# Expert outputs scattered by addition into one memory row per token, with a fence op, a ring of eight and rows cleared by copies

## What is computed

```
x = layernorm(x + self_attention(x))            # 16 heads, one shared key and value head
x = layernorm(x + cross_attention(x, context))  # one head, additive mask
x = layernorm(x + ffn(x))                       # 8 experts, the best 2 for each token

ffn:  scores = softmax(x @ Wg.T);  the two largest, divided by their sum, are the weights comb
      for each expert e:  h = x @ W1[e].T + b1[e];  a, b = split(h)
                          g = a * sigmoid(b)                       # 512 numbers per token
                          out += (g @ Wo.T + bo) * comb[e]
```

## Time and profile before

| | before |
|---|---|
| median of 3 runs | 1420.98 us |
| the profiled execution, its own time | 1420.46 us |
| its span, first to last instruction | 1418.7 us |
| busy: PE, DVE, ACT, POOL | 1274.8, 1147.8, 747.3, 642.5 us |
| moved by DMA | 237.57 MB, mean 167 GB/s |
| mean granted clock of TensorE | 0.974 |

### The profile page before, as it was taken

How to read it: one execution, slowest core, us unless ns; L and a number is a source line. 1 busy time by engine, 2 the same in 40 slices (tenths; PEclk the granted TensorE clock), 3 DMA queues, 4 the chain that set the end, 5 groups by cost and what they waited for, 6 DMA issues and landing times.

```text
span 1418.7 us, 30148 instructions
## 1 busy us (share of the span) xinstructions
PE 1274.8 (90%) x7734; PEld 900.7 (63%) x7735; DVE 1147.8 (81%) x3145; ACT 747.3 (53%) x1740; POOL 642.5 (45%) x978
## 2 busy tenths in 40 slices
PE   6997999999999999999988569999999999968886
PEld 4443555655556555555553357888888888858886
DVE  0565889898888988988986658888888888869998
ACT  1245777777777787777776212233233223314444
POOL 3011354455444554555445323333333333348886
PEclk9998999999999999999999679999999999989999
DMA  7656667667676675775655853433443344379995
GB/s 163 166 111 125 113 151 172 149 163 149 158 157 140 146 163 135 157 138 145 157 129 195 290 215 129 135 130 129 134 135 129 130 134 135 133 271 330 332 335 194
DMA packets 182817, 237.57 MB, mean 167 GB/s; under 512 B 21376, under 2 KB 144256, under 8 KB 176960
## 3 DMA queue, kind: packets, MB, share of 16 engines
q1 hardware_dynamic: 158864, 169.50, 47.3%
q0 software_dynamic: 17488, 55.02, 10.3%
q10 hardware_dynamic: 6368, 11.89, 2.4%
HBM read 138.34 MB, written 98.30 MB: 167 GB/s over the span
## 4 chain that ended last, share of the span: by engine, by line
PE 62%; DVE 17%; issue 9%; DMA 5%; ACT 4%; POOL 1%; SPq 1%; DVEq 0%; ACTq 0%; POOLq 0%
PE psO L623 6%; PE psS L730 5%; PE psHb L1399 5%; PE psHb L1396 5%; PE psHb L1395 4%; PE psHa L1395 4%; PE psHa L1396 4%; PE psHa L1399 4%; PE psB L652 4%; PE psT L740 4%; DVE negmax L1031 3%; DVE x2in L1591 3%; PE psX L1419 2%; DVE gt_lo L1567 2%; PE psA L612 2%
## 5 line engine op out<-in xcount | busy, mean ns | idle before, releaser
L1031 DVE TENSOR_REDUCE negmax<-psS 128x2 f32<-128x512 f32 x512 | 350.7, 688 | 94.6 <-PE psS L730 77.0
L870 ACT ACTIVATE probs<-psT 128x512 f32<-128x512 f32 x512 | 304.0, 599 | 161.0 <-PE psT L740 143.3
L1476 ACT ACTIVATE sig<-hb 128x512 f32<-128x512 f32 x135 | 85.6, 634 | 286.6 <-DVE hb L1549 286.6
L730 PE MATMUL psS<-kstack,qstack 96*128 96x256 bf16 x1024 | 195.2, 273 | 31.3 <-DVE kstack L1129 15.6
L740 PE MATMUL psT<-qstack,kstack 99*128 99x512 bf16 x512 | 194.8, 383 | 4.4 <-ACT probs L870 4.3
L1358 POOL DMA_INDIRECT g_rows<-g,slot x135 | 134.7, 998 | 69.8 <-issue 66.5
L730 PEld LDWEIGHTS psS<-kstack,qstack 96*128 96x128 bf16 x1024 | 93.1, 104 | 90.2 <-DVE negmax L1031 27.4
L482 POOL DMA_INDIRECT lists<-x,slots x128 | 128.6, 1005 | 33.9 <-issue 30.1
L623 PE MATMUL psO<-probs,vaug 128*32 128x512 f32 x1024 | 139.1, 616 | 0.4 <-ACT probs L870 0.4
L1560 DVE SCALAR_TENSOR_TENSOR g<-g,xe,sig 128x512 f32<-128x512 f32 x135 | 101.5, 752 | 26.0 <-DVE g L1556 16.6
L1549 DVE TENSOR_TENSOR hb<-psHb,b 128x512 f32<-128x512 f32 x135 | 93.4, 692 | 33.1 <-issue 28.9
(11 more groups left out here) (207 smaller groups left out, 2956.4 us busy)
## 6 DMA issues: line engine op xcount, KB each, us to landing
rows<-g_rows SPq DMA_DIRECT2D x32, 1024.0 KB, 8.1
qstack<-q_parts SPq DMA_DIRECT2D x192, 128.0 KB
xe<-lists SPq DMA_DIRECT2D x135, 133.0 KB, 2.1
q_parts<-qpart SPq DMA_DIRECT2D x32, 384.0 KB
sums<-x SPq DMA_DIRECT2D x32, 264.0 KB
x2in<-sums SPq DMA_DIRECT2D x32, 264.0 KB, 4.7
xt<-in_x_t SPq DMA_DIRECT2D x32, 256.0 KB
part_raw<-in_f_t SPq DMA_DIRECT2D x32, 256.0 KB, 5.0
```

The source lines that it names most:

```text
L730: last = mm(psS[:, u % 2, hh * S:(hh + 1) * S], qstack[0:KROWS, b1.s4, 2 * hp + hh, c * P:(c + 1) * P], kstack[0:KROWS, b1.s4, :], start=T ...
L870: nc.scalar.activation(probs[:, u % PT, :], psT[:, u % 2, :], ACT.Exp, scale=SELF_SCALE).then_inc(sm["exp_done"], 1)
L1031: v.tensor_reduce(negmax[:, b1.s2, 2 * hp:2 * hp + 2, c], psS[:, u % 2, :].rearrange("p (h k) -> p h k", h=2), AX.X, ALU.max, negate=True) ...
```

## The change

`g_rows` has one row per token now, and the scatter of a tile adds to it (`compute_op=ALU.add`) in place of overwriting it. From this follow the other parts:

1. The column with the first expert goes (`ROW` is `D + E + 1`), and with it the DVE copy L1160, POOL's `away` and DVE's wait for it. `slot` is a plain copy of the row number.
2. Two tiles of different experts can hold the same token. POOL waits before the scatter of tile o: for o = 1 to 7 until the scatters of the three tiles before it have landed, later only where the expert changes (`turn_tab`, 16 at such a tile and 0 otherwise, is loaded into a register and added to the number waited for). After the waits POOL runs a `fence` op on one column, then the scatter.
3. The rows must be zero at first. POOL clears a 128 x 512 tile `zeros`, SP writes it 4 times (1 MB) to `zero_rows` in step 0 of the attention stage, and ACT issues 20 copies of 1 MB from there to `g_rows`, one in unit 15 of each of the steps 6 to 25.
4. `xe` gets a ring of 8, and the loops of the tile stage are written out for 8 tiles in place of 4.
5. In the pair stage SP loads 512 KB of `rows` per pair, POOL adds nothing, and PE transposes `rows` itself.

The diff, cut to its core:

```
-            pool.iota(x2[:, s, :, D + E], pattern=[[2 * P, QC]], base=2 * s * S, channel_multiplier=2,
+            pool.iota(x2[:, s, :, D + E], pattern=[[P, QC]], base=s * S, channel_multiplier=1,
...
             if t.fixed and t.n == 0:
                 load_setup()
+                sp.wait_ge(dram["zeros_made"], 1)
+                sp.dma_start(dram["zero_rows"].rearrange("(p k) h -> p k h", p=P),
+                             zeros[:, :].unsqueeze(1).to_broadcast([P, ZROWS, zeros.shape[1]])
+                             ).then_inc(dram["zeros_stored"], 16)
...
+        def clear_rows(t):
+
+            places = dram["g_rows"].rearrange("(p k) h -> p (k h)", p=P)
+            width = ZROWS * dram["g_rows"].shape[1]
+            n = t.n - 6
+            if 0 <= n < places.shape[1] // width:
+                act.wait_ge(dram["zeros_stored"], 16)
+                act.dma_start(places[:, n * width:(n + 1) * width], dram["zero_rows"].rearrange("(p k) h -> p (k h)", p=P)
+                              ).then_inc(dram["rows_cleared"], 16)
...
+                if u == 15:
+                    clear_rows(t)
...
-                v.tensor_copy(x2[:, b6.s2, :, D + E + 1], topf[:, b6.s2, :, 0]).then_inc(sm["comb_ready"], 1)
...
             if active(t):
-                wait(sp, "g_ready", done(t.back(4)))
+                wait(sp, "g_ready", done(t.back(8)))
...
-            if active(t):
-
-                wait(pool, f"xe_loaded{t.s4}", ring(t) + 16)
+            turn = None
+            for m in range(1, 4):
+
+                before = o.back(m)
+                if active(o) and (not o.fixed or o.n >= 8):
+                    turn = pool.value_load(turn_tab[0:1, bass.ds(o.n, 1)], min_val=0, max_val=16) if turn is None else turn
+                    wait(pool, f"g_stored{before.s4}", ring(before) + turn)
+                elif active(o) and before.n >= 0:
+                    wait(pool, f"g_stored{before.s4}", ring(before) + 16)
+            if active(o):
                 wait(pool, "g_ready", done(o))
-                pool.tensor_tensor(away[:, t.s4:t.s4 + 1], xe[:, t.s4, FIRST:FIRST + 1],
-                                   expf[:, bass.ds(t.n, 1)], ALU.subtract).then_inc(sm["away_ready"], 1)
+                wait(pool, "fenced", done(o.back(4)))
+                pool.tensor_tensor(fence[:, o.s4:o.s4 + 1], zero[:, :], zero[:, :], ALU.add).then_inc(sm["fenced"], 1)
             if active(o):
                 pool.indirect_dma_start(out=dram["g_rows"], out_offset=bass.IndirectOffsetOnAxis(
-                    ap=slot[:, o.s4:o.s4 + 1], axis=0), in_=g[:, o.s4], in_offset=None
+                    ap=slot[:, o.s4:o.s4 + 1], axis=0), in_=g[:, o.s4], in_offset=None, compute_op=ALU.add
                     ).then_inc(sm[f"g_stored{o.s4}"], 16)
...
-            if active(t, PAIRS):
-                wait(pool, f"rows_loaded{t.s4}", ring(t) + 16)
-                for c in range(QC):
-                    wait(pool, "g_transposed", QC * t.n + c - 3)
-                    pool.tensor_tensor(row_sum[:, t.s2 * QC + c], rows[:, t.s4, c, 0:H], rows[:, t.s4, c, H:2 * H], ALU.add
-                                       ).then_inc(sm["rows_added"], 1)
...
                 if active(t, PAIRS):
-                    wait(pe, "rows_added", QC * t.n + c + 1)
+                    if c == 0:
+                        wait(pe, f"rows_loaded{t.s4}", ring(t) + 16)
...
-                v.scalar_tensor_tensor(slot[:, i.s4:i.s4 + 1], away[:, i.s4:i.s4 + 1], 0.0, xe[:, i.s4, ID:ID + 1],
-                                       ALU.not_equal, ALU.add)
+                v.tensor_copy(slot[:, i.s4:i.s4 + 1], xe[:, i.s8, ID:ID + 1])
...
-            "g_rows": nc.dram_tensor("g_rows", (2 * (T + 2 * E * P), H2 // 2), F32, kind="Internal").ap(),
+            "g_rows": nc.dram_tensor("g_rows", (T + 2 * E * P, H2 // 2), F32, kind="Internal").ap(),
+            "zero_rows": nc.dram_tensor("zero_rows", (4 * P, H2 // 2), F32, kind="Internal").ap(),
```

More of the change, by code:

```diff
@@ L70, in s4, with n, s8, back @@
         return self.r % 4
+class Tile(Step):
+    @property
+    def n(self):
+        return 8 * self.j + self.r
+    @property
+    def s8(self):
+        return self.r % 8
+    def back(self, k):
+        return Tile(self.j, self.r - k)
 def attention(nc, ctx, io, dram):
@@ L112, in attention @@
     rden = sb("rden", [P, 2, QC * 8])
-    with nc.sbuf_tensor("pad", [P, 2 * E, ROW], F32) as pad:
+    ZROWS = 4
+    with nc.sbuf_tensor("pad", [P, 2 * E, ROW], F32) as pad, nc.sbuf_tensor("zeros", [P, dram["g_rows"].shape[1]], F32) as zeros:
         pass
@@ L445, in expert_constants @@
             number, listbase, upper = dram["number"], dram["listbase"], dram["upper"]
+            pool.memset(zeros[:, :], 0.0).then_inc(dram["zeros_made"], 1)
             pool.memset(pad[:, :, :], 0.0).then_inc(sm["pool_chain"], 1)
@@ L1198, in experts @@
     I32 = mybir.dt.int32
-    rows, row_sum, x2in, y, result = (dram[k] for k in ("rows", "row_sum", "x2in", "y", "result"))
+    rows, x2in, y, result = (dram[k] for k in ("rows", "x2in", "y", "result"))
     w1_hi, w1_lo, b1, bo = dram["w1_hi"], dram["w1_lo"], dram["b1"], dram["bo"]
@@ L1215, in experts @@
         pass
+    with nc.sbuf_tensor("g", [P, 4, H], F32) as g:
+        pass
     past = sb("past", [P, TILES, E])
@@ L1221, in experts @@
     exp_tab = sb("exp_tab", [P, TILES], I32)
+    turn = sb("turn", [P, TILES])
+    turn_tab = sb("turn_tab", [P, TILES], I32)
     pad_tab = sb("pad_tab", [P, E], I32)
[L1224 to L1225 removed]
+    xe = sb("xe", [P, 8, ROW])
     sig = sb("sig", [P, 2, H])
@@ L1228, in experts @@
     xet_lo = sb("xet_lo", [P, 2, DC * P], F32R)
-    away = sb("away", [P, 4])
+    fence = sb("fence", [P, 4])
+    zero = sb("zero", [P, 1])
     slot = sb("slot", [P, 4], U32)
@@ L1267, in ring, with ring8 @@
     def ring(i):
-        return 16 * (i.j + i.r // 4)
+        return 16 * ((2 if isinstance(i, Tile) else 1) * i.j + i.r // 4)
+    def ring8(i):
+        return 16 * (i.j + i.r // 8)
     def active(i, count=TILES):
@@ L1274, in pipeline @@
     def pipeline(eng, step):
-        for r in range(8):
-            step(Step(0, r))
-        with eng.Fori(2, TILES // 4) as j:
-            for r in range(4):
-                step(Step(j, r))
-        for r in range(TILES % 4 + 3):
-            step(Step(TILES // 4, r))
+        for r in range(16):
+            step(Tile(0, r))
+        with eng.Fori(2, TILES // 8) as j:
+            for r in range(8):
+                step(Tile(j, r))
+        for r in range(TILES % 8 + 3):
+            step(Tile(TILES // 8, r))
     def pair_pipeline(eng, step):
@@ L1327, in load_rows @@
         def load_rows(t):
-            wait(sp, "rows_added", done(t.back(4), QC))
+            wait(sp, "g_transposed", done(t.back(4), QC))
             sp.dma_start(rows[:, t.s4], stored_rows[bass.ds(t.n, 1)].rearrange("o p c h -> (o p) c h")
@@ L1415, in step @@
             if active(t):
-                wait(pe, f"xe_loaded{t.s4}", ring(t) + 16)
+                wait(pe, f"xe_loaded{t.s8}", ring8(t) + 16)
                 wait(pe, "xet_split", done(t.back(2)))
                 for k in range(DC):
-                    last = nc.tensor.transpose(psX[:, t.s2, k * P:(k + 1) * P], xe[:, t.s4, k * P:(k + 1) * P],
+                    last = nc.tensor.transpose(psX[:, t.s2, k * P:(k + 1) * P], xe[:, t.s8, k * P:(k + 1) * P],
                                                ident[:, :])
@@ L1429, in step @@
                         lambda: None).then_inc(sm["a_product"], 1)
-            if active(i) and active(t) and t.r % 4 != 3:
+            if active(i) and active(t) and t.r % 8 != 7:
                 ahead.append(load_expert(t))
@@ L1451, in pair_step @@
                         last = nc.tensor.transpose(psG[:, c, k * P:(k + 1) * P],
-                                                   row_sum[:, t.s2 * QC + c, k * P:(k + 1) * P], ident[:, :])
+                                                   rows[:, t.s4, c, k * P:(k + 1) * P], ident[:, :])
                     last.then_inc(sm["g_transposed"], 1)
@@ L1650, in decoder_layer @@
             place("w1_hi", [P, W1], F32R)
-            with (nc.sbuf_tensor("rows", [P, 4, QC, 2 * H], F32) as rows, nc.sbuf_tensor("row_sum", [P, 4, H], F32) as row_sum,
+            with (nc.sbuf_tensor("rows", [P, 4, QC, H], F32) as rows,
                   nc.sbuf_tensor("x2in", [P, 4, QC, D + E], F32) as x2in, nc.sbuf_tensor("y", [P, 4, QC, D], F32) as y):
-                dram.update(rows=rows, row_sum=row_sum, x2in=x2in, y=y)
+                dram.update(rows=rows, x2in=x2in, y=y)
             place("w1_lo", [P, W1], F32R)
```

42 lines of the change are left out of this document (24 added, 18 removed).

## The result

The changed kernel takes 1404.43 us (median of 9 runs, 1401.26 to 1411.38), the kernel before 1417.77 us in the same comparison (9 runs, 1409.81 to 1421.96): ratio 0.991, 95% interval 0.989 to 0.993. The prediction was 1404 us. The profiled execution of after took 1407.59 us (span 1405.2), 12.9 us less than that of before. The total is close; its terms are less so.

A forecast was written before the change was run, and what follows sets the result against it. PE bounds the tile stage; DVE, held by POOL's additions, the pair stage. From 1420.5 us, -27.7 - 2 + 8 + 6 - 1 = -16.7 gives 1404 us; own range 1394 to 1415, range leaving out two in ten 1387 to 1425.

The forecast's parts named there:

- Pair stage, -27.7: Pair stage: without POOL's additions DVE's L1591 shortens and PE becomes the bound at 1.87 us a block: -27.7 us.
- the rival that blamed the traffic: Pair stage: busy DMA, not POOL, slows L1591, so DVE stays at 4.67 us a pair: 1431 us, chance 0.05.
- Hand-over, -2: Last scatter to pair stage: half the bytes -1.6, one row_sum less -1.4, later landing +1.1; together -2 us.
- First eight tiles, +8: Tile stage start: each scatter waits for the one before to land, 5.1 us apart against 3.02: +8 us.
- The seven changes of expert, 0: Tile stage after tile 8: waits remain only at seven expert changes, each delaying one scatter by 2 us: 0.
- Adding, steady, 0: Steady tile stage: scatters with doubled or tripled DMA time still fit in 3.02 us, up to 3.8 times: 0.
- Clearing copies' issue, +6: Attention stage: each of 20 issues holds ACT about 0.54 us, some 0.3 of which reach PE: +6 us.
- The rival of a collision at 1436: Attention stage: clearing copies get ahead of the query loads in 10 of 20 steps, +32: 1436 us, chance 0.09.
- Ring of eight, -1: Tile stage: the ring of 8 removes at most 2.1 us of PE's waits for tiles: -1 us.
- zeros, 0: Program start: writing 1 MB of zeros takes about 4 us before the first queries are stored: 0, at most +4.

The follow-up runs named there:

- b1: Kernel before, but GpSimd adds nothing in the pair stage and PE transposes the first half of each loaded row: 1390.4 us, ratio 0.981.
- b4: Kernel before with its full loads, but GpSimd adds the first half of each row to itself: 1402.4 us, ratio 0.992.
- d2: Changed kernel, plus GpSimd adding the two different rows of each loaded pair into a tile nobody reads: 1430.5 us, ratio 1.013.
- a2: Changed kernel with a scatter that overwrites and does not add, all waits kept: 1389.2 us, ratio 0.979.
- c1: Changed kernel, but the table of turns also decides the waits for tiles 1 to 7: 1390.8 us, ratio 0.981.
- d1: Changed kernel, plus GpSimd adding each loaded row to itself into a tile nobody reads: 1417.5 us, ratio 1.002.

## Why the prediction was right, and where only its sum was

- **Pair stage, -27.7: right.** From the third block's transposes to the last's are 115.2 us (1278.90 to 1394.06) where I had 114.1 and before has 141.8: -26.6. From first transpose to the end it is 130.5 us (1274.67 to 1405.2) against 157.5: -27.0. Mechanism, place and next bound (PE at 1.87 us a block) were as written, and b1, b4 and d2 show the cause; the rival that blamed the traffic is refuted.
- **Hand-over, -2: too much.** From last scatter to first transpose 10.6 us became 10.4. The 6.2 us from the request on did shrink to 3.3 (-2.9, predicted -3.0). The landing took 2.7 us more, where I had put 1.1 between bounds of 0 and 2; a2's 4.1 us shows that adding is what lengthens it. A part may come from the wait ahead of the first spare tile, behind which the last three scatters follow at 1.95 us: in c1, where they follow at 1.96 and 2.48, it is 6.3 us instead of 7.1. No run separates the two.
- **First eight tiles, +8: right in kind, 9.9 in size.** The mis-sized step was "I take 4.4 for the adding one": it was 4.9 to 5.2. The reading itself was not sound either: 4.4 is what passes from the very last scatter to SP's next request, and a2 shows 2.8 to 3.0 for most scatters early in the stage. Too long a figure for the plain scatter stood in for an adding one that is nearly twice as long. That the term came out within 2 us is therefore in part luck.
- **The seven changes of expert, 0: right for seven, but the waits are eight.** "From a scatter's start to the slot that needs it are 9 us" holds in the middle: in c1, which has only those waits, DVE never waited for a slot. The eighth wait, ahead of the first spare tile, was missing from the count. It lies three tiles from the end, where no later tile can make up for it: c1's stage is 2.0 us over before.
- **Adding, steady, 0: right.** 2.8 times the engine time, under the 3.8 from which it would decide.
- **Clearing copies' issue, +6: wrong.** The step that failed is "an issue holds ACT for about 0.54 us", read from one transfer with a cast behind it. That row names PE's `psHa` as what released the cast, which I had read past; it shows a cast that began after an issue, not one that was held by it. Here the same kind of issue lies beside an exponential. The rival of a collision at 1436 did not come about: with the clearing in place the kernel was no slower.
- **Ring of eight, -1, zeros, 0:** too small to be seen in the spread of the start.

By the three stretches of the first table the prediction said +6, +7 and -29.7, and the profiles show +1.7, +11.9 and -27.2. Too much by 4.3 in the first stretch stood against too little by 4.9 and 2.5 in the others, so the spans differ by 13.5 us where I had 16.7. That these errors nearly cancel is luck: the +6 rested on a wrong reading, and the +1.7 that came is no effect of the change that can be shown. That the timed median still lies within 0.5 us of the forecast is luck too: the rest is owed to the median of before, which was 3.2 us lower in this comparison than the 1420.98 that I started from.

## What to carry to other kernels

When one engine's instruction with two SBUF operands is long only beside another engine's, ask when the other one ends: here the whole gain of 27 us came from taking away 2.7 us of GpSimd work per pair, on an engine that was not the bound. Count the turns in a table by where the kernel waits, not by what the table stands for: spare tiles at the end can bring one more. A wait for a DMA's landing is cheap alone and dear in series: price it as landing plus issue against the loop's period, and let data decide where it is needed, in the first iterations too. For a DMA issue read from a trace, check that the engine's next instruction was really held by it.

## What the runs showed of the hardware that I had not expected

- An indirect DMA that adds took GpSimd 1.56 us to issue instead of 0.99 (after and a2). In the waits of the first tiles it had landed 4.9 to 5.2 us after its start where most plain ones had after 2.8 to 3.0, and it took 61.5% instead of 21.1% of the DMA engines' time for about the same bytes. The tile stage's pace stayed at 3.02 us.
- A VectorE scalar_tensor_tensor with both tensors in SBUF that began beside one of GpSimd's additions ended 0.28 or 0.29 us after that addition, or after its own 0.48 us where these ran longer, whatever the addition's length (before, b4, d1, d2; in before 59 of 60).
- GpSimd's addition of 128x512 took 1.04 us with one operand read twice (b4) and 1.26 us with two (before) where neither of those VectorE instructions ran beside it. As the second of a pair it mostly took 1.35 and 1.47 us.
- A DMA issue of 0.50 us on ScalarE's queue ran beside an activation without moving the next one (after).
